# A decoder layer on one core: subtracting softmax maxima through free rows of existing products, and one 154-column cross score product per row group

## What is computed

```python
x = x + attn(layernorm(x), ...)           # score = q k^T / 16, softmax over 256 keys
x = x + xattn(layernorm(x), ctx, mask)    # score = q k^T / 4, softmax over 77 keys
x = x + soft_moe(layernorm(x), ...)       # logits, dispatch, gelu(slots @ w1) @ w2, combine
```

## Time and profile before

| | |
|---|---|
| median of 3 runs | 1773.68 us (1773.43 to 1777.49) |
| span of the profiled execution | 1770.5 us |
| TensorE busy | 1735.7 us, 98% |
| VectorE / ScalarE / GpSimd busy | 1158.1 / 1018.4 / 439.5 us |
| mean granted TensorE clock | 0.999 of 2.4 GHz |

### The profile page before, as it was taken

How to read it: one execution, slowest core, us unless ns; L and a number is a source line. 1 busy time by engine, 2 the same in 40 slices (tenths; PEclk the granted TensorE clock), 3 DMA queues, 4 the chain that set the end, 5 groups by cost and what they waited for, 6 DMA issues and landing times.

```text
span 1770.5 us, 40859 instructions
## 1 busy us (share of the span) xinstructions
PE 1735.7 (98%) x17306; PEld 1570.7 (89%) x17306; DVE 1158.1 (65%) x2307; ACT 1018.4 (58%) x1775; POOL 439.5 (25%) x354
## 2 busy tenths in 40 slices
PE   8999999999999999999999999999999999999998
PEld 7779798998989888898988989898898988989988
DVE  4656576675867667676666867667576666765453
ACT  4445756566656656656565655656655655655553
POOL 2112122222223122222222313222222313222232
PEclk9999999999999999999999999999999999999999
DMA  5000000000000000000000000000000000000000
GB/s 163 10 1 10 2 10 8 10 8 2 16 1 10 7 10 8 2 16 2 10 8 8 10 2 10 8 10 7 1 16 2 10 8 10 8 1 7 2 7 7
DMA packets 20852, 19.67 MB, mean 11 GB/s; under 512 B 9920, under 2 KB 19776, under 8 KB 20288
## 3 DMA queue, kind: packets, MB, share of 16 engines
q1 hardware_dynamic: 20672, 17.06, 3.5%
HBM read 12.86 MB, written 4.19 MB: 10 GB/s over the span
## 4 chain that ended last, share of the span: by engine, by line
PE 85%; ACT 5%; DVE 4%; issue 4%; POOL 1%; DMA 0%; POOLq 0%; SPq 0%; DVEq 0%; ACTq 0%
PE ps L465 21%; PE ps L466 19%; PE ps L467 19%; PE ps L590 3%; PE ps L573 2%; PE ps L553 2%; PE ps L775 2%; PE ps L700 2%; PE ps L620 2%; PE ps L843 2%; PE ps L665 1%; PE ps L766 1%; POOL h_lo L1446 1%; PE ps L872 1%; ACT L1034 1%
## 5 line engine op out<-in xcount | busy, mean ns | idle before, releaser
L1446 POOL TENSOR_TENSOR h_lo<-h_f,h_hi 128x512 fp32r<-128x512 f32 x256 | 336.9, 1324 | 1052.7 <-DVE h_hi L1329 1052.7
L465 PE MATMUL ps<-sl_hi,w_hi 128*128 128x256 f32 x1024 | 304.9, 298 | 5.4 <-DVE sl_lo L1088 2.9
L465 PE MATMUL ps<-w_hi,h_hi 128*128 128x256 f32 x1024 | 300.9, 294 | 5.5 <-POOL h_lo L1446 5.3
L466 PE MATMUL ps<-w_hi,h_lo 128*128 128x256 f32 x1024 | 290.1, 283 | 0.0
L467 PE MATMUL ps<-w_lo,h_hi 128*128 128x256 f32 x1024 | 289.8, 283 | 0.0
L466 PE MATMUL ps<-sl_hi,w_lo 128*128 128x256 f32 x1024 | 288.8, 282 | 0.0
L467 PE MATMUL ps<-sl_lo,w_hi 128*128 128x256 f32 x1024 | 288.8, 282 | 0.0
L465 PEld LDWEIGHTS ps<-sl_hi,w_hi 128*128 128x128 f32 x1024 | 194.4, 190 | 28.9 <-ACT h_f L1034 14.2
L1329 DVE CAST h_hi<-h_f 128x512 fp32r<-128x512 f32 x256 | 175.4, 691 | 67.1 <-ACT h_f L1034 66.3
L1034 ACT ACTIVATE h_f<-ps 128x512 f32<-128x512 f32 x256 | 151.2, 598 | 104.6 <-PE ps L467 103.6
L465 PEld LDWEIGHTS ps<-w_hi,h_hi 128*128 128x128 f32 x1024 | 196.0, 191 | 15.0 <-POOL h_lo L1446 11.3
(11 more groups left out here) (213 smaller groups left out, 4217.8 us busy)
## 6 DMA issues: line engine op xcount, KB each, us to landing
x<-in_x SPq DMA_DIRECT2D x16, 256.0 KB, 2.7
out<-acc SPq DMA_DIRECT2D x16, 256.0 KB, 2.2
g_w<-in_w SPq DMA_DIRECT2D x2, 1024.0 KB, 12.2
cx<-in_ctxT SPq DMA_DIRECT2D x16, 77.0 KB, 2.0
g_wqk<-in_wqk SPq DMA_DIRECT2D x1, 1024.0 KB, 6.8
g_se<-in_se SPq DMA_DIRECT2D x1, 1024.0 KB, 8.7
biases<-in_bias SPq DMA_DIRECT2D x1, 640.0 KB, 5.1
mk_i<-in_mask SPq DMA_DIRECT2D x16, 38.5 KB
```

The costliest lines, as they stand in the source:

```text
L465: te.matmul(o, lhs[0], rhs[0], start=first, stop=False)
L466: te.matmul(o, lhs[1], rhs[0], start=False, stop=False)
L1446: Q_.tensor_tensor(h_lo[:, part, :], h_f[:, part, :], h_hi[:, part, :].bitcast(f32), ALU.subtract)\
```

## The change

The row maxima no longer have products of their own. In self-attention the query of the second product is no longer `qs` but `qz`, whose second 16 rows are zero (made by a new ScalarE operation in `qh`); `k_lo` gets ones in rows 16 and 17 of each group (a new ScalarE operation in `kh`, and another form of `kl`). `mx.n` writes the rounded maximum and its rest side by side in `md` (two small VectorE operations instead of one), so that `mt.n` puts them on rows 16 and 17, and `sh.n` adds them to `qz`. `mh.n` is gone, and so are the third products of `shifted.n`. In `shifted2.c` the keys `kms2` (made by GpSimd in `km`) have a one in a free row, and `sh2.c` writes a copy of the query with the maximum in that row; `mh2.c` and the matmuls of L688 are gone. `mx2.c` writes its two maxima per group straight into `md2` by two reductions, without a copy. `scores2.c` takes both parities in one moving operand of 154 columns: 8 fp32 matmuls instead of 16. The orders of all engines are new; the bank lists are now read off TensorE's order. START's TensorE list has 167 idle matmuls instead of 197.

The diff, cut (of START the first lines alone, of ORDER TensorE's, VectorE's and GpSimd's):

```diff
--- before.py
+++ after.py
...
     pe="""
-        m.lt.0 l.outer.3.0 d.kv m.dispatch.0 l.outer.3.1 c.xt.1 m.slots.0 l.comb.3 d.xt.2 c.k c.q d.q2 c.v
-        m.hidden.0.0 d.scores2.0 m.hidden.0.1 m.hidden.0.2 d.mt2.0 m.hidden.0.3 m.lt.1 l.combine.3 d.shifted2.0
-        m.outer.0.0 c.scores.0 m.dispatch.1 m.outer.0.1 c.mt.0 m.slots.1 m.comb.0 c.shifted.0 d.pv2.0 m.hidden.1.0
-        d.scores2.1 m.hidden.1.1 m.hidden.1.2 d.mt2.1 m.hidden.1.3 m.lt.2 m.combine.0 c.pv.0 d.shifted2.1 m.outer.1.0
-        d.tr2.0 m.dispatch.2 c.scores.1 d.pv2.1 m.slots.2 d.ob2.0 m.comb.1 m.outer.1.1 c.mt.1 m.hidden.2.0
-        c.shifted.1 d.tr2.1 m.hidden.2.1 c.scores.2 c.pv.1 m.hidden.2.2 d.ob2.1 m.hidden.2.3 m.lt.3 c.mt.2
-        m.combine.1 d.oproj2 c.shifted.2 m.dispatch.3 c.tr.0 m.outer.2.0 c.ob.0 c.scores.3 c.pv.2 m.slots.3 m.comb.2
-        c.mt.3 m.outer.2.1 c.shifted.3 m.hidden.3.0 d.xt.3 m.combine.2 m.hidden.3.1 m.hidden.3.2 c.pv.3 m.hidden.3.3
-        d.logits.0 c.tr.1 d.logits.1 d.logits.2 c.ob.1 d.logits.3 c.oproj
+        m.lt.0 l.outer.3.0 d.kv m.dispatch.0 l.outer.3.1 c.xt.1 m.slots.0 l.comb.3 d.xt.2 c.k c.q d.q2 m.hidden.0.0
+        c.v m.hidden.0.1 m.hidden.0.2 d.scores2.0 m.hidden.0.3 m.lt.1 d.mt2.0 l.combine.3 d.shifted2.0 m.outer.0.0
+        c.scores.0 m.dispatch.1 m.outer.0.1 c.mt.0 m.slots.1 m.comb.0 c.shifted.0 d.pv2.0 m.hidden.1.0 m.hidden.1.1
+        c.pv.0 d.scores2.1 m.hidden.1.2 m.hidden.1.3 m.lt.2 d.mt2.1 m.combine.0 d.shifted2.1 d.tr2.0 m.outer.1.0
+        m.dispatch.2 d.pv2.1 c.scores.1 m.slots.2 m.comb.1 m.outer.1.1 c.mt.1 m.hidden.2.0 d.ob2.0 c.shifted.1 d.tr2.1
+        m.hidden.2.1 c.scores.2 c.pv.1 m.hidden.2.2 d.ob2.1 m.hidden.2.3 m.lt.3 c.mt.2 m.combine.1 c.shifted.2
+        d.oproj2 m.dispatch.3 m.outer.2.0 c.tr.0 m.slots.3 c.ob.0 c.scores.3 c.pv.2 m.comb.2 m.outer.2.1 c.mt.3
+        m.hidden.3.0 c.shifted.3 d.xt.3 m.combine.2 m.hidden.3.1 c.pv.3 m.hidden.3.2 c.tr.1 m.hidden.3.3 c.ob.1
+        d.logits.0 d.logits.1 d.logits.2 d.logits.3 c.oproj
...
+        m.cm.0 d.mask m.edn.0 d.stats.2 c.stats.1 d.kv c.xh.1 m.ds.0 d.xh.2 c.xt.1 m.row_max l.cb.3 d.xt.2 m.sl.0 c.qd
+        c.v m.hid.0.0 c.kd l.pr.3 m.hid.0.1 m.hid.0.2 d.mx2.0 m.cm.1 m.hid.0.3 d.sh2.0 l.acc.3 c.kl c.qs m.edn.1
+        c.mx.0 m.ds.1 l.finish c.sh.0 m.sl.1 m.cb.0 m.hid.1.0 m.hid.1.1 m.pr.0 d.mx2.1 m.hid.1.2 m.cm.2 d.sh2.1
+        m.hid.1.3 m.acc.0 m.keep m.edn.2 d.nrm2.0 m.ds.2 c.mx.1 m.cb.1 m.sl.2 c.sh.1 d.nrm2.1 m.pr.1 m.hid.2.0
+        m.hid.2.1 c.mx.2 c.sh.2 m.hid.2.2 m.cm.3 m.acc.1 m.hid.2.3 m.edn.3 d.x2 m.ds.3 d.stats.3 c.nrm.0 d.xh.3 c.mx.3
+        m.cb.2 m.sl.3 c.sh.3 m.pr.2 d.xt.3 m.acc.2 m.hid.3.0 m.hid.3.1 c.nrm.1 m.hid.3.2 d.xs m.hid.3.3 c.x1
     """,
...
     pool="""
-        c.rstd.1 d.rstd.2 c.bias.1 d.bias.2 m.hid.0.0 m.hid.0.1 m.hid.0.2 m.hid.0.3 m.hid.1.0 m.hid.1.1 m.hid.1.2
-        m.hid.1.3 m.hid.2.0 m.hid.2.1 m.hid.2.2 m.hid.2.3 d.rstd.3 m.hid.3.0 m.hid.3.1 m.hid.3.2 m.hid.3.3
+        c.rstd.1 d.rstd.2 m.hid.0.0 d.km m.hid.0.1 m.hid.0.2 m.hid.0.3 m.hid.1.0 m.hid.1.1 m.hid.1.2 m.hid.1.3
+        d.bias.2 m.hid.2.0 m.hid.2.1 m.hid.2.2 m.hid.2.3 d.rstd.3 m.hid.3.0 c.bias.1 m.hid.3.1 m.hid.3.2 m.hid.3.3
     """,
...
+        s0.idle.10 s0.idle.2 c0.xt.1 s0.idle.6 c0.k c0.q c0.v s0.idle.18 s0.idle.3 c0.scores.0 s0.idle.8 s0.idle.3
+        c0.mt.0 s0.idle.1 c0.shifted.0 s0.idle.8 c0.scores.1 c0.pv.0 s0.idle.7 c0.mt.1 s0.idle.1 c0.shifted.1
+        s0.idle.7 c0.scores.2 c0.pv.1 s0.se_transp.0.0 s0.idle.5 c0.mt.2 c0.shifted.2 c0.tr.0 s0.idle.3 c0.ob.0
...
+        s0.hi.0 s0.hi.1 c0.xt.1 c0.k c0.q c0.kh c0.qh s0.hi.2 s0.se_squares c0.ex.0 c0.xo.0 c0.ex.1 c0.xo.1
...
+        c0.stats.1 s0.lo.0 c0.xh.1 c0.xt.1 s0.columns s0.lo.1 c0.kd d0.mask c0.qd c0.v c0.kl c0.qs c0.mx.0 s0.gammas
...
-                    for keys, first in ((k_hi, True), (k_lo, False)):
+                    for queries, keys, first in ((qs, k_hi, True), (qz, k_lo, False)):
                         for i in range(R):
                             rows = slice(32 * i, 32 * i + 32)
-                            last = te.matmul(ps[:, 1 + i, t * S:(t + 1) * S], qs[rows, n, t * P:(t + 1) * P],
+                            last = te.matmul(ps[:, 1 + i, t * S:(t + 1) * S], queries[rows, n, t * P:(t + 1) * P],
                                              keys[rows, n, :], start=first, stop=not first)
...
-                    for keys, first in ((k_hi, True), (k_lo, False)):
+                    for queries, keys, first in ((qs, k_hi, True), (qz, k_lo, False)):
                         for i in range(R):
                             rows = slice(32 * i, 32 * i + 32)
-                            te.matmul(ps[:, 1 + i, j * S:(j + 1) * S], keys[rows, n, j * P:(j + 1) * P], qs[rows, n, :],
-                                      start=first, stop=False)
-                    for i in range(R):
-                        rows = slice(32 * i, 32 * i + 32)
-                        last = te.matmul(ps[:, 1 + i, j * S:(j + 1) * S], ones[rows, :], sh[rows, :],
-                                         start=False, stop=True)
+                            last = te.matmul(ps[:, 1 + i, j * S:(j + 1) * S], keys[rows, n, j * P:(j + 1) * P],
+                                             queries[rows, n, :], start=first, stop=not first)
                 last.then_inc(s["st_ps"], 1)
 
...
+                for t in range(NT):
+                    for i in range(R):
+                        rows = slice(32 * i, 32 * i + 32)
+                        last = te.matmul(ps[:, 1 + i, 2 * t * CTX:2 * (t + 1) * CTX], q2[rows, c, t * P:(t + 1) * P],
+                                         km2[rows, c, :, :].rearrange("p e k -> p (e k)"), start=False, stop=t == NT - 1)
+                last.then_inc(s["s2_ps"], 1)
...
-                        at = (2 * e + t) * CTX
-                        for i in range(R):
-                            rows = slice(32 * i, 32 * i + 32)
-                            last = te.matmul(ps[:, 1 + i, at:at + CTX], q2[rows, c, t * P:(t + 1) * P],
-                                             km2[rows, e, c, :], start=False, stop=(e, t) == (1, NT - 1))
...
                 pe.wait_ge(s["sh2"], nth("sh2", a, c + 1))
+                if c == 0:
+                    pe.wait_ge(s["kms2"], nth("kms2", a, 1))
                 for e in range(2):
                     for i in range(R):
                         rows = slice(32 * i, 32 * i + 32)
-                        te.matmul(ps[0:CTX, 1 + i, e * S:(e + 1) * S], km2[rows, e, c, :], q2[rows, c, :],
-                                  start=True, stop=False)
-                    for i in range(R):
-                        rows = slice(32 * i, 32 * i + 32)
-                        last = te.matmul(ps[0:CTX, 1 + i, e * S:(e + 1) * S], ones[rows, 0:CTX], sh2[rows, e, :],
-                                         start=False, stop=True)
+                        last = te.matmul(ps[0:CTX, 1 + i, e * S:(e + 1) * S], kms2[rows, c, e, :], sh2[rows, e, :],
+                                         start=True, stop=True)
                 last.then_inc(s["st2_ps"], 1)
 
...
             def qh_step(a):
                 act.wait_ge(s["q_d"], nth("q_d", a, 1))
                 act.wait_ge(s["v_ps"], nth("v_ps", a, 1))
+                nc.scalar.activation(qz[:, :, :], q_d[:, :, :], ACT.Identity, scale=half[:, 0:1]).then_inc(s["q_z"], 1)
                 copy(q_hi[:, :, :], q_d[:, :, :]).then_inc(s["q_h"], 1)
...
-                act.wait_ge(s["mt_ps"], nth("mt_ps", a, n + 1))
-                copy(mh[:, :], ps[:, 0, 0:S]).then_inc(s["mh"], 1)
+                act.wait_ge(s["k_h"], nth("k_h", a, 1))
+                nc.scalar.activation(k_d[:, :, :], k_d[:, :, :], ACT.Identity, scale=half[:, 0:1], bias=half[:, 3:4])\
+                    .then_inc(s["k_m"], 1)
...
+                dve.wait_ge(s["q_z"], nth("q_z", a, 1))
...
-                dve.wait_ge(s["k_h"], nth("k_h", a, 1))
-                minus(k_lo[:, :, :], k_d[:, :, :], k_hi[:, :, :]).then_inc(s["k_lo"], 1)
+                dve.wait_ge(s["k_m"], nth("k_m", a, 1))
+                V.scalar_tensor_tensor(k_lo[:, :, :], k_hi[:, :, :].bitcast(f32), half[:, 2:3], k_d[:, :, :],
+                                       ALU.mult, ALU.add).then_inc(s["k_lo"], 1)
...
-                V.tensor_copy(md[:, :, :, 0:32:HD], mx[:, n, :, :].rearrange("p i t -> p t i").unsqueeze(3).broadcast_to([P, NT, R, 2])).then_inc(s["md"], 1)
+                top = mx[:, n, :, :].rearrange("p i t -> p t i")
+                V.tensor_copy(md[:, :, :, HD].bitcast(f32r), top).then_inc(s["md_hi"], 1)
+                dve.wait_ge(s["md_hi"], nth("md_hi", a, n + 1))
+                V.tensor_tensor(md[:, :, :, HD + 1], top, md[:, :, :, HD], ALU.subtract).then_inc(s["md"], 1)
 
             def sh_step(a, n):
 
-                dve.wait_ge(s["mh"], nth("mh", a, n + 1))
-                V.scalar_tensor_tensor(sh[:, :], mh[:, :].bitcast(f32), cols[:, NMASK:NMASK + 1], ps[:, 0, 0:S],
```

(32 more changed lines are left out.)

264 lines of the change are left out of this document (118 added, 146 removed).

## The result

The changed kernel takes 1763.1 us (median of 4 runs, 1761.2 to 1763.4) against 1775.3 us for the kernel before, measured beside it (1773.4 to 1777.5): ratio 0.9927, 95% interval 0.9914 to 0.9939. It is faster by 0.7%, where I had forecast 1.6%; the time lies 3 us above my range. The profiled execution has a span of 1761.6 us, 8.9 less than before. Its time from outside is 1763.4 us, 1.8 us more than its span, and so it is in every execution on record. The 3.2 us that I took for this difference compared the median before with the span of a faster execution (1770.5 us); that is also why the medians differ by 12.2 us and the spans by 8.9.

What follows compares the result with a forecast made beforehand. It took TensorE's matmul stream (98% busy) as the bound: 1770.5 - 15.4 - 8.0 - 12.2 + 8 + 0 = 1742.9 us of span, with 3.2 us to the timed execution 1746 us. Range 1734 to 1760 us.

Steps and rivals of the forecast that it cites:

- Part 1: Self-attention shifted step: dropping the third product's 512 matmuls saves 15.4 us on TensorE, bounds 14.7 to 16 us.
- Part 2: Cross shifted step: fewer matmuls save 0.25 us in each of 32 steps, 8.0 us, ends 7.5 and 8.6 us.
- Part 3: Cross score product with 154 columns: a set at 0.14 us saves 12.2 us, ends 7.7 and 15 us.
- Part 4: Other engines' work in the loop: new waits lose 0.6 us a pass, 8 us in 13 passes, ends 0 and 17.
- my three waits: TensorE waits per pass: 0.3 to 0.6 us at `shifted2.0`, 0 to 0.4 at `outer.1.0`, 0 to 0.5 more at `dispatch.3`.
- Part 5: START: beyond the cheaper products, gains and losses of 3.2 us cancel to 0; ends 4 us better, 5 us worse.
- way to the first scores: START: `kh` and `qh` ahead of `qs` cost 1.35 us, the earlier `s0.lo.0` 1.8 us, together 3.2 us.
- waited-for sets: START: some eight self sets 0.5 us shorter, two cross sets about 1.2 us each; 6.4 us, 3.2 already counted.
- A: Rival, chance 0.16: waits in the loop grow to what the products free; over 104.5 us a pass, 1755 to 1765 us.
- D: Rival, chance 0.07: all savings arrive, no new wait in the loop, START as planned; 1730 us.
- the two marks: One pass of ORDER under 103.2 us or over 104.5 us would show the forecast wrong; 103.8 us was forecast.
- My chain to `shifted2.0`: In the loop, from the end of `m.hidden.0.3`: 2.6 to 2.9 us against 2.3 us of TensorE's cover.

Runs made afterwards that it cites:

- e5: The changed kernel with the cross score product as 16 matmuls of 77 columns a step instead of 8 of 154: 1773.8 us, ratio 0.9987.
- e4: The changed kernel's new products with START, ORDER and FINISH all in the old order: 1770.7 us, ratio 0.9977.
- e6: e4 with `c.kh` moved behind `m.ge.0.2` in ScalarE's ORDER, instead of ahead of `m.ge.0.1`: 1760.5 us, ratio 0.9911.
- e8: e3 with `c.sh.2` moved behind `m.hid.2.2 m.cm.3` in VectorE's ORDER: 1748.0 us, ratio 0.9839.
- e13: e3 with `m.edn.3` moved ahead of `m.hid.2.3` in VectorE's ORDER: 1751.3 us, ratio 0.9878.
- e10: e1 with `c1.scores.2 c1.pv.1` ahead of `m0.dispatch.0` on TensorE in START, and 6 idle matmuls there instead of 12: 1754.6 us, ratio 0.9894.
- e1: The changed kernel with `d0.mask` put back behind `s0.lo.3` in START's VectorE list: 1753.1 us, ratio 0.9883.
- e3: The changed kernel with START's four lists in the old order, ORDER and FINISH staying new: 1746.8 us, ratio 0.9843.
- e12: e9 with the splits of the first weights put back behind the first transposes on VectorE and ScalarE: 1743.5 us, ratio 0.9830.
- e2: The kernel before with `d0.mask` moved forward between `c0.kd` and `c0.qd` in START's VectorE list: 1785.1 us, ratio 1.0061.
- e9: The changed kernel with START's new lists up to `d0.logits.3` (mask step put back) and the old lists from there on: 1745.5 us, ratio 0.9841.
- e11: The kernel before, with old products, START and FINISH, given the new ORDER: 1783.9 us, ratio 1.0061.
- e7: e1 with 26 more idle matmuls on TensorE in three long waits of START: 1755.2 us, ratio 0.9881.

## Why the prediction was wrong, step by step

**Part 1** (shifted step, 15.4 us): 0.68 us a step instead of 0.92, as forecast. **Part 2** (cross shifted step, 8.0 us): 1.03 us instead of 1.27, so 0.24 x 32 = 7.7 us, inside the bounds.

**Part 3** (154 columns, 12.2 us): right in kind, a little too high. The step takes 0.62 us, a set of four records 0.155 us where I took 0.14: the price in proportion to the four 256-column records at 0.25 us gives 0.15. The saving is 0.32 x 32 = 10.2 us, of which e5 shows about 9 to arrive. Of the two rules cited there from the Trainium skill (TensorE: Matmul & The Clock Gate, LDWEIGHTS and Wait, 56ns, not 53.3ns?) neither gives this number: the weight load of 107 ns, as I read it, would have left the set near 0.12 us and saved 13 to 15 us, and N / 2.4 GHz + 2.5 ns a matmul would have saved nothing, against the 10.2 us measured. Here the rows decide.

**Part 4** (new waits in the loop, +8 us): wrong, and the sentence that failed is "the reordering as such gives nothing there". I counted changes of tiling on TensorE and three waits, but did not ask what the old ORDER would do with the new products. e4 shows it: they free 2.1 us a pass on TensorE, and waits take 1.9 of it back, 0.8 us through `kh` alone (e6). The new ORDER puts `hidden.0.0` ahead of `c.v`, the first gelu ahead of `qh` and the next two ahead of `kh`; I had seen only the delay of the fourth, behind `kh`. Of my three waits, the one at `shifted2.0` came out at 0.17 us instead of 0.3 to 0.6, and the 0.18 us at `outer.0.0` went; `outer.1.0` has none. The one at `dispatch.3` came with the size I gave (0.46 us after `oproj2` more than `oproj2` takes) and with another cause: not `cm.3` behind `sh.2` (e8) but `acc.1`, `hid.2.3` and `edn.3` in series (e13). The two operations that `qh` and `kh` gained take 1.15 and 1.24 us, not 1.06, and the two of `km` 0.86 us each, not a microsecond in all. Rows 9 also left out a third wait of the passes before, 0.17 us in front of `hidden.2.2` for a gelu, which is still there after. So a pass is 103.37 us, not 103.8: 5 us better than forecast in 13 passes.

**Part 5** (START, net 0 beyond the products): the step that broke the forecast. The way to the first scores was 3.2 us by my sum and is 11.0. Without the mask step in it my sum holds: the first scores are 3.3 us later than before in e10, and 4.0 in e1 with its lower clock at 11 to 15 us. The chain through `kh` and `qh` is 1.4 us longer (from `c0.k` to the first scores 10.0 us in e3, e10 and e12 against 8.6 before), as I said, and the early splits cost about 1.5 us (e12). What I left out, and so put at nothing, was `d0.mask`: it stood in the diff of VectorE's list, in the line I was reading for `s0.lo.0`, and I took a step that had waited for nothing at 52 us to wait for nothing at 17. VectorE stood there for 8.9 us. Its cost is 8.1 us in the traces and 10.0 in the medians (e1), 11.1 in the kernel before (e2). Second, I followed START only to the first scores and took the rest as a count of waited-for sets. The chain of a set did shorten as computed: `mt` to `shifted` is 0.93 us in e9 (28.26 to 29.19) against 1.40. But the second half with the new order is 10.3 us longer (e9 against e1), of which some 3.4 us are the lower clock; which of its moved steps cost the rest stays open. Third, the gain of the waited-for sets was too high: from `c0.scores.0` to `m0.lt.0` it is 88.7 us in e9 against 91.4, so 2.6 us, where six self sets at 0.5 and two cross sets at 1.2 give 5.4.

**The sum.** START -5.4 forecast, +17.3 measured; ORDER -20.8 and -26.0; FINISH -1.3 and -0.2. Had START kept its old order, the forecast would have met the median by two errors of opposite sign: START 6.1 us worse than forecast and ORDER 5.7 us better (e3); FINISH was 1.1 us worse, and the step from span to time, 1.8 us instead of 3.2, gives 1.4 back.

**Rivals.** None of A to D was it. The time lies in A's 1755 to 1765 us, but by chance: A's mechanism, waits in the loop that grow to what is freed, wanted more than 104.5 us a pass. D's loop (below 103.2 us a pass, no new wait) came nearest, with 103.37. The pass even stayed between the two marks at which I had called the forecast wrong; there was no such mark for the end of START. The range was too narrow for one reason: every bound in it was a bound on a term that I had, and START's other 23 us had no term.

## What to carry to other kernels

When a diff rewrites the order of a queue, list every step that moved, also those that have nothing to do with the change, and for each that moved forward ask which transfer or engine it waits for at its new time; a step may show no wait in the trace of before only because it came late enough. Cost a new order against the old order with the new durations, not against the old kernel: here the new products alone saved 0.2% (e4), the new ORDER alone cost 0.6% (e11), and together they saved 1.6% (e3). And in a stretch where one chain is waited for, such as a pipeline's start, a saving elsewhere doesn't count until the chain has been followed to the end of that stretch.

## What the runs showed of the hardware

**The granted clock fell for some microseconds after TensorE had stood still, and also where it was two thirds or four fifths busy, there not always.** Windows of the kernel after, columns as in e7:

```profile
25.00:30.00 5.00, 0.00 (x0) 0.00 (x0) 3.56 (x9) 2.14 (x3) 0.00 (x0) 0.60 0.22 42
30.00:35.00 5.00, 3.40 (x26) 3.21 (x27) 3.41 (x2) 3.67 (x17) 1.25 (x1) 0.50 0.02 4
```

TensorE does nothing from 25 to 30 us (its wait ahead of the first scores is 9.24 us), and when it starts again its clock is at 0.50, that is 1.2 GHz, and its first matmuls take 0.58 us instead of 0.39. In FINISH, with the same lists and nearly the same work in the window, the clock fell in one execution and not in another (e1 first, then e7):

```profile
1685.00:1695.00 10.00, 8.13 (x69) 7.89 (x67) 8.58 (x17) 5.80 (x12) 5.38 (x4) 1.00 0.08 28
```

```profile
1685.00:1695.00 10.00, 8.12 (x59) 7.88 (x59) 8.70 (x17) 4.94 (x10) 5.38 (x4) 0.88 0.08 26
```

FINISH is 3.0 us longer in e7 than in e1, and e7 has a second such stretch (clock 0.79 from 1738 to 1746 us, 1.00 in e1). The executions of the kernel before go from 1772.2 us at a mean clock of 0.999 to 1778.9 us at 0.996, in step with the clock: most of what looks like noise in this kernel goes with how much of the time the clock was low. What decides it in the stretches where TensorE is busy in part stays open.

**ScalarE loads a table for the gelu (1.28 us).** In the rows of e4 the load stands between `q_hi` and the first gelu. The copies `k_hi` and `k_d` between two gelus bring no further one, so moving them costs only their own time. My chain to `shifted2.0` holds no load: it begins at the last gelu of the expert, and the load stands ahead of the first.
